# Attention kernel with top-2 experts: routing spread between the maxima of attention, map entries and the transposition of the maxima placed elsewhere

## The reference, cut to what matters

```python
xn = layernorm(x)                                   # x: [4, 1024, 256]
# attention: 16 heads of 16, causal, ALiBi bias, softmax
q, k, v = xn @ Wq, xn @ Wk, xn @ Wv
scores = (mask(q @ k.T) + slope * (j - i)) / sqrt(16)
attn = (softmax(scores) @ v) @ Wo + bo
# router: two experts of eight for each token
r = xn * rsqrt(mean(xn**2) + 1e-6) * 256**-0.5 * router_scale
logits = r @ router_logits
probs = softmax(logits);  choices = top_2(logits)
weights = probs / sum(probs of the two)
# experts: rows sorted by expert, gelu(x @ gate) * (x @ up), @ down, times per-expert scale
out = x + attn + sum_k weights[k] * expert[choices[k]](xn)
```

## Time and profile before

| | us |
|---|---|
| median of 3 runs (931.12 to 932.04) | 931.17 |
| the profiled execution | 941.12 |
| its span | 939.4 |
| TensorE busy, share of the span | 812.5, 86% |
| VectorE | 562.1, 60% |
| ScalarE | 483.2, 51% |
| GpSimd | 390.0, 42% |

### The profile page before, as it was taken

How to read it: one execution, slowest core, us unless ns; L and a number is a source line. 1 busy time by engine, 2 the same in 40 slices (tenths; PEclk the granted TensorE clock), 3 DMA queues, 4 the chain that set the end, 5 groups by cost and what they waited for, 6 DMA issues and landing times. The chain is left out here.

```text
span 939.4 us, 17505 instructions
## 1 busy us (share of the span) xinstructions
PE 812.5 (86%) x5618; PEld 426.3 (45%) x5619; DVE 562.1 (60%) x1560; ACT 483.2 (51%) x1011; POOL 390.0 (42%) x456
## 2 busy tenths in 40 slices
PE   5989601799999999999999999856999999999598
PEld 2555400134444444444444444313555656555497
DVE  4767364988888888888888888301222222222177
ACT  2333300067777777777777777852333333333374
POOL 3545340033223233322323332323666666665398
PEclk9999855589999999999999999996999999999799
DMA  4999899295555666555566600009222222222485
GB/s 157 221 263 269 213 107 121 34 253 74 62 61 57 82 81 81 67 62 61 59 82 81 81 3 3 2 6 321 86 84 84 84 84 84 84 85 78 129 245 182
DMA packets 115004, 100.32 MB, mean 107 GB/s; under 512 B 58172, under 2 KB 95676, under 8 KB 114876
## 3 DMA queue, kind: packets, MB, share of 16 engines
q1 hardware_dynamic: 105976, 80.50, 46.9%
q0 software_dynamic: 8960, 18.95, 6.4%
HBM read 63.89 MB, written 35.00 MB: 105 GB/s over the span
## 5 line engine op out<-in xcount | busy, mean ns | idle before, releaser
L784 ACT ACTIVATE probs<-spsum 128x512 f32<-128x512 f32 x576 | 312.1, 604 | 169.6 <-PE spsum L835 163.8
L742 DVE CUSTOM_DVE_ANT_0 junk<-mpsum,mask 128x128 bf16<-128x128 f32 (+7 forms) x512 | 360.0, 754 | 58.5 <-issue 51.7
L824 PE MATMUL mpsum<-ks,qs 102*128 102x512 bf16 (+3 forms) x768 | 183.5, 343 | 45.9 <-DVE cpsum L731 26.3
L722 POOL TENSOR_SCALAR_AFFINE_SELECT probs<-probs 128x512 f32<-128x512 f32 x128 | 78.8, 634 | 340.8 <-ACT probs L784 340.8
L835 PE MATMUL spsum<-qs,ks 105*128 105x512 bf16 (+3 forms) x768 | 199.2, 329 | 10.6 <-ACT probs L784 8.3
L855 PE MATMUL cpsum<-probs,vs 128*17 128x256 f32 (+2 forms) x2560 | 152.7, 360 | 1.5 <-POOL probs L722 0.8
L1037 PE MATMUL gu<-w_gu,xTs 128*128 x288 | 139.2, 607 | 1.7 <-ACT xTs L981 1.7
L1016 DVE COPY hT<-hp 128x256 f32<-128x256 f32 x72 | 30.6, 425 | 167.8 <-PE hp L1044 100.6
L824 PEld LDWEIGHTS mpsum<-ks,qs 102*128 102x128 bf16 x768 | 69.8, 100 | 122.5 <-DVE maxima L742 39.8
L835 PEld LDWEIGHTS spsum<-qs,ks 105*128 105x128 bf16 x768 | 67.1, 97 | 102.9 <-ACT probs L784 52.9
L956 POOL DMA_INDIRECT expert_rows<-y,places x72 | 70.7, 983 | 72.2 <-ACT y L990 42.2
(11 more groups left out here) (124 smaller groups left out, 698.5 us busy)
## 6 DMA issues: line engine op xcount, KB each, us to landing
qk_parts<-parts SPq DMA_DIRECT2D x32, 384.0 KB, 4.4
qs<-qk_parts SPq DMA_DIRECT2D x96, 128.0 KB
ks<-qk_parts SPq DMA_DIRECT2D x96, 128.0 KB
yk<-expert_rows SPq DMA_DIRECT2D x32, 256.0 KB, 3.1
v_rows<-vt SPq DMA_DIRECT2D x32, 136.0 KB, 4.5
vs<-v_rows SPq DMA_DIRECT2D x16, 272.0 KB, 12.0
x_in<-in_x SPq DMA_DIRECT2D x8, 512.0 KB, 6.3
xn_rows<-xn SPq DMA_DIRECT2D x8, 512.0 KB, 5.8
```

Source lines behind the costliest of these rows:

```text
L722: pool.affine_select(out=part, in_=part, compare_op=ALU.is_ge, fill=0.0, base=0, pattern=[[0, 4], [1, P]], channel_multiplier=-1).then_inc ...
L742: last = dve.tensor_tensor_reduce(junk[:, slot, c:c + w], mpsum[:, slot, c:c + w], keep["mask"][:, S - w:S], 1.0, 3 * NEG, ALU.add, ALU.ma ...
L784: act.activation(probs[:, u % PRING, h], spsum[:, (4 * u + h) % SRING], ACT.Exp, scale=SCALE).then_inc(exp_done, 1)
L824: last = pe.matmul(mpsum[:, slot, at + c:at + e], qs[hq][0:R_MAX, h, qt * P:(qt + 1) * P], ks[hq][0:R_MAX, h, c:e], start=True, stop=True)
```

## The change

The block `route` is gone; its parts stand elsewhere.

- Projection: no hardware loop, four x buffers instead of two, one store of v per chunk for all quads, and the scale of the logits is computed per chunk by GpSimd (three more small operations) and applied by ScalarE. GpSimd sets up the constants of the routing and the mask between its first and second chunk. SyncE loads the constant rows of all quads at the start, and the first quad in pieces behind the stores of chunks 2 to 5.
- Attention: VectorE takes one piece of the routing after the item of each odd pair: 49 pieces, 45 in steps 0 to 4 and 4 in step 5. The counts are an item of their own in pair 10 of step 1 and are copied out of PSUM. ScalarE takes its exponential ahead of unit 5 of step 1.
- The transposed maxima go into a buffer of the ring of scores, not of maxima, once per step; a score that comes later to that buffer waits for `t_taken`.
- GpSimd writes the map in steps 5 to 12, two DMAs behind each of units 6, 7, 8 and 0, straight from the kept tiles. SyncE loads `w_gu` in eight parts in the same steps (its place holds the routing's tiles until then, which is why they are printed as `w_gu` below) and reads the map back at the end of attention.

```diff
+COUNT_AT = (1, 10)
+SOFTMAX_AT = (1, 5)
+MAP_FROM = 5
+MAP_UNITS = (6, 7, 8, 9)
...
+def score_slots():
+    p, = [p for p, pair in enumerate(PAIR_ITEMS) if (1, NI - 1) in pair]
+    seq = [("T", 0)] + [("S", 0, h) for h in range(4)]
+    for n in range(1, B * NQ * NU):
+        t, j = (n - 1) // NU, (n - 1) % NU + 1
+        for h in range(4):
+            seq.append(("S", n, h))
+            if p // 2 + 1 == j and 2 * (p % 2) == h and t + 1 < B * NQ:
+                seq.append(("T", t + 1))
+    return seq, {user: i for i, user in enumerate(seq)}
...
-                for q in range(NQ):
-                    sp.dma_start(scratch["v"][q].rearrange("(t p) w -> p t w", p=P)[:, ds(4 * c, 4), :],
-                                 vt[:, par, :, q].rearrange("p t h w -> p t (h w)")).then_inc(v_stored[par], 16)
+                sp.dma_start(scratch["v"].rearrange("(t p) w -> p t w", p=P)[:, 4 * c:4 * c + 4, :],
+                             vt[:, par].rearrange("p t q h w -> p t (q h w)")).then_inc(v_stored[par], 16)
...
+            for c in range(NC):
+                stores(c, c % 2, c + XR < NC)
+                if c == 2:
+                    sp.wait_ge(parts_stored[0], 16 + 16 * 2)
+                if 2 <= c < 5:
+                    load_rows(sp, scratch, heads, 0, 0, (2 * c - 4, 2 * c - 3))
+                if c == 5:
+                    for i in range(2):
+                        sp.wait_ge(v_stored[i], 16 * 2)
+                    load_values(sp, scratch, heads, 0, 0)
...
+            load_quad(sp, scratch, heads, 0, 1)
             maxima_rows(0, 0)
+            load_quad(sp, scratch, heads, 0, 2)
...
+                if t == MAP_FROM:
+                    sp.wait_ge(routed, 1)
+                if MAP_FROM <= t < MAP_FROM + NE:
+                    e = t - MAP_FROM
+                    sp.dma_start(keep["w_gu"][:, e * DH:(e + 1) * DH], ins["w_gu"][:, e * DH:(e + 1) * DH]).then_inc(keep["w_gu_in"], 16)
...
-                    if j == LOW_LAST[0]:
-                        map_entries(b, hq)
+                    if j in MAP_UNITS and t >= MAP_FROM:
+                        map_entries(NU * t + j, len(MAP_UNITS) * (t - MAP_FROM) + MAP_UNITS.index(j))
...
+            def map_entries(n, part):
+                wait_apart(pool, exp_done, 4 * n + SRING)
+                wait_apart(pool, routed, 1)
+                for e in range(2 * part, min(2 * part + 2, 2 * NT)):
...
+                def then(ins_):
+                    ins_.then_inc(dve_step, 1)
+                    steps[0] += 1
+                    dve.wait_ge(dve_step, steps[0])
...
+                for p in range(PAIRS):
+                    if (t, p) == COUNT_AT:
+                        count_item()
+                    for j, k in PAIR_ITEMS[p]:
                         if has(j):
                             item(t + j, (hq + j) % NQ, k)
+                    if p % 2 == 1:
+                        next(route, None)
```

More of the change, by code:

```diff
@@ L38 @@
 NC = TOK // CH
+XR = 4
 NST = 2 * TOK // P + NE
@@ new lines, in load_quad, with __init__, __call__ @@
+def load_quad(sp, scratch, heads, b, hq):
+    load_rows(sp, scratch, heads, b, hq, range(len(Q_PART)))
+    load_values(sp, scratch, heads, b, hq)
+class Room:
+    def __init__(self, buffer):
+        self.words, self.at = buffer, 0
+    def __call__(self, shape, dt=F32):
+        n = math.prod(shape[1:]) // (2 if dt is BF16 else 1)
+        part = self.words[0:shape[0], self.at:self.at + n]
+        self.at += n
+        if dt is not F32:
+            part = part.bitcast(dt)
+        dims = "abcde"[:len(shape) - 1]
+        return part.rearrange(f"p ({' '.join(dims)}) -> p {' '.join(dims)}", **dict(zip(dims, shape[1:])))
@@ L192, in project @@
         passed = sem("passed1")
-        x_loaded = [sem(f"x_loaded{i}") for i in range(2)]
+        x_loaded = [sem(f"x_loaded{i}") for i in range(XR)]
         x_stored = [sem(f"x_stored{i}") for i in range(2)]
@@ L243, in _ @@
             sp.dma_start(w_qk[:, :, :, :], ins["w_qk"]).then_inc(weights_in, 16)
-            sp.dma_start(x_in[:, 1], x_rows[1]).then_inc(x_loaded[1], 16)
+            for i in range(1, XR):
+                sp.dma_start(x_in[:, i], x_rows[i]).then_inc(x_loaded[i], 16)
             def stores(c, par, load):
@@ L621, in attend @@
         mparts = sb("mparts", [12 * KT, 2, P], BF16)
-        entries = sb("entries_now", [P, 2, 2, 2, 2], I32)
-        slots = sb("slots", [P, 2, 2, 2], I32)
+        room, early = keep["w_gu_room"], keep["route"]
+        rank_of, tile_no, reset, ones, tri = (early[name] for name in ("rank_of", "tile_no", "reset", "ones", "tri"))
+        logit, escale = keep["logits"][:, :, :], keep["escale"]
+        hit, key, masked_l, expd, prob, picked = (room([P, NT, NE]) for _ in range(6))
+        chosen = [room([P, NT, NE]) for _ in range(2)]
+        cnt, run, pos = (room([P, NE, NT]) for _ in range(3))
+        both = room([P, NT, NE], BF16)
+        counts = [room([P, NT * NE]) for _ in range(2)]
+        past = room([1, NST, NE])
+        first, esum, renorm, guard, sk, slot_f = (room([P, NT]) for _ in range(6))
+        top, pk = ([room([P, NT]) for _ in range(2)] for _ in range(2))
+        slot_i = room([P, 3, NT], I32)
+        total, tiles, ends, base = (room([P, NE]) for _ in range(4))
+        total_i, tiles_i = (room([P, NE], I32) for _ in range(2))
+        tile_f = room([1, NST])
         mpsum = ctx.enter_context(nc.psum_tensor("mpsum", [P, 2, S], F32))
@@ L641, in attend @@
         ctx_taken = sem("ctx_taken")
-        entries_in = [sem(f"entries_in{i}") for i in range(2)]
-        entries_out = [sem(f"entries_out{i}") for i in range(2)]
+        entries_out = sem("entries_out")
+        dve_step = sem("dve_step_r")
+        shifted = sem("shifted")
+        exp_ready = sem("exp_ready")
+        both_ready = sem("both_ready")
+        routed = sem("routed")
         block = ctx.enter_context(nc.Block())
@@ L759, in _, with count_item @@
+            def count_item():
+                n = ITEM_NO[COUNTS]
+                dve.wait_ge(m_taken, n + 1)
+                wait_apart(dve, m_ready, n + 1)
+                for j in range(2):
+                    last = dve.tensor_copy(counts[j], mpsum[:, n % RING, CH * j:CH * j + NT * NE])
+                last.then_inc(m_taken, 1)
+            route = routing()
             for k in range(NI - 1):
@@ new lines, in item, with score_buffer, count_item @@
+                last.then_inc(m_ready, 1)
+            def score_buffer(*user):
+                i = SCORE_AT[user] - SRING
+                if i >= 0 and SCORE_SEQ[i][0] == "T":
+                    pe.wait_ge(t_taken, SCORE_SEQ[i][1] + 1)
+                elif i >= 0:
+                    pe.wait_ge(exp_done, 4 * SCORE_SEQ[i][1] + SCORE_SEQ[i][2] + 1 + SRING)
+            def count_item():
+                n = ITEM_NO[COUNTS]
+                pe.wait_ge(both_ready, 1)
+                pe.wait_ge(m_taken, n + 1)
+                for j, which in enumerate((tri, ones)):
+                    last = pe.matmul(mpsum[:, n % RING, CH * j:CH * j + NT * NE], which, both,
+                                     start=True, stop=True)
+                last.then_inc(m_ready, 1)
@@ L935, in _ @@
             sp.sem_inc(y_free, RR)
-            sp.dma_start(places[:, :, :].rearrange("p s c -> p (s c)"), scratch["map"].rearrange("(p s) c -> p (s c)", p=P)).then_inc(places_in, 16)
             for e in range(NE):
```

446 lines of the change are left out of this document (203 added, 243 removed).

## The result

| | before | after |
|---|---|---|
| median, beside each other (4 runs each) | 931.61 | 894.89 |
| from, to | 931.12 to 932.3 | 894.28 to 897.78 |
| ratio, 95% interval | | 0.9604 (0.9586 to 0.9622) |
| the profiled execution | 941.12 | 894.28 |
| its span | 939.4 | 892.5 |

The forecast was 902.0 us (885 to 914), the result 894.89. The profiled execution of before lay 10 us above its other runs, that of after lies among its own; so the two spans differ by 46.9 us and the medians by 36.7. Chips differ too: the runs that follow were made in three sets, each on one chip, and the kernel before took 938.08, 941.81 and 935.03 us in them.

The account below looks back on a forecast made before the run. TensorE's order was taken to bound the kernel, its two holes being the quick gains. Terms -42.5 - 1.9 + 15 + 7.2 + 0 - 6.9 were summed to -29.2: profiled 911.9, median 902 us, range 885 to 914.

Parts of the forecast that it names:

- the hole: Between projection and attention: 48.0 us, mostly routing alone on VectorE, become 5.5, so -42.5 us.
- routing: Attention steps 0 to 5: pieces want 38.1 us of VectorE, 23.1 fit its idle time, so +15 us.
- map entries: Steps 5 to 12: entry pairs delay the mask of unit 1, TensorE waits 0.9 us eight times, +7.2 us.
- the stretch behind attention: Attention to experts: -3.8 entries landing earlier, -2.1 gather not behind map load, -1 gather before weights; -6.9 us.
- the projection: Projection: four x buffers remove VectorE's wait, -2.6; GpSimd's late reciprocal root costs about 0.7; -1.9 us in all.
- The bound of 12.3 us for the first quad: Projection: upper bound on what loading the first quad there costs in DMA time; 0 was taken.
- the handover of 0.33 us: Routing steps: each of 49 pieces delays the next VectorE item by 0.33 us, read behind the transposition.
- Rival B: Steps 0 to 5: handovers vanish, routing's 21.9 us fit in 23.1 of idle time; 887 us, chance 13%.
- Pieces in contention with masks: Routing steps: two-input VectorE pieces slowed by GpSimd masks, some 2 us more; counted as nothing.
- rival C: Steps with map entries: masks come in time, as pairs are shorter or TensorE has slack; 895 us, chance 13%.
- The transposition: Each attention step: freeing the maxima buffer removes TensorE's 0.92 us wait, but VectorE starts no earlier; 0 us.
- wait of about 0.9 two items later: Attention steps: sign that TensorE's wait behind the transposition only moves two items later, about 0.9 us.

## Why the prediction was right, and where it was wrong

The range held, and that is in part luck: the forecast's error of 7.1 us is what is left of two larger ones that point in opposite directions. By the profiled spans the sum should have been -29.2 (its terms add up to -29.1) and was -46.9, a miss of 17.7 us, more than the 17 us from the forecast to the range's lower end. Against it, the 9.95 us by which the profiled execution of before exceeded its median were carried over to the kernel after, whose profiled execution has no such surplus (894.28 against a median of 894.89). The largest term, the hole, was right in mechanism and size; routing, map entries and the stretch behind attention were not.

| term | forecast | by the traces |
|---|---|---|
| between projection and attention | -42.5 | -44.3 |
| projection (last logits at 107.94) | -1.9 | -2.1 |
| routing, steps 0 to 5 | +15 | +7.9 (0.6 and 7.3) |
| entries and transposition, steps 6 to 13 | +7.2 | -3.2 |
| steps 14 and 15 | 0 | -1.1 |
| behind attention | -6.9 | -2.1 |
| experts and combination | 0 | -2.1 |

*The hole and the projection* held. The bound of 12.3 us for the first quad was empty: its cost was 0 and, had it been left at attention's start, 15.3.

*Routing*: the step that failed is the handover of 0.33 us. That row stands behind the transposition, where VectorE's sequencer executes two increments between the wait and the item; behind a piece it executes one, and that handover measured 0.22. With that the sum's own working gives 21.2 + 0.84 + 49 x 0.22 = 32.8 us into 23.1, +9.7, near the +7.9. The mechanism was right: without the handovers 8.8 us come back. Rival B, which wanted them hidden, was wrong about them; the work without them does fit. Pieces in contention with masks, which the sum left at nothing, added nearly nothing: two of them met one (the one at 266.48 took 0.90 us instead of 0.42, one at 153.81 took 0.75), 0.8 us in all, but the 21.10 of the earlier trace rows held such a meeting too, and the busy time is 21.2.

*Map entries*: the mechanism was right, a weight load of TensorE waits for the late mask of unit 1. The step that failed is the time from the mask of unit 7 to that of unit 1, forecast as 10.1 to 10.6 us and measured as 9.8. The pairs took 2.24 as forecast; the changes between mask and pair were shorter, a mask following an entry in 0.02 us and not in 0.16. TensorE lost 0.17 us a step, not 0.9: rival C, on that chip. On the other chip a step with entries took 0.83 us more than there, and by its rows with another mechanism than the one forecast.

*The transposition*: 0 in the routing steps, 0.25 us in each other step of the changed kernel, and nothing measurable in the time of either kernel. The reason given (VectorE does not start earlier) is what the traces show for the items; the "wait of about 0.9 two items later" came as 0.70.

What remains of the shorter steps (27.11 against 27.52, while 0.25 are the transposition's and the entries cost 0.17) is about the wait of 0.23 to 0.30 us for an exponential that stood in each of the steps 1 to 13 of before:

```profile
262.74 0.39 PE L835 MATMUL spsum<-qs,ks 105*128 105x512 bf16 x1 [0.28 <-ACT probs L784]
```

In the steps of after it doesn't stand, with the transposition in its old buffer either. But it is not the change's alone: in the kernel before with only the transposition moved it is absent on one chip (steps of 26.95) and 0.12 to 0.17 us on the other (27.24 to 27.29), and in the kernel before on that other chip mostly 0.12 to 0.21. What sets it was not isolated.

*Behind attention*: the step that failed is -3.8 for the landing of the last entries. Something did hold the block until 4 us after ScalarE's end, but it was GpSimd's drain, which the change leaves in place; the wait of 4.3 us at that barrier in the earlier trace rows was put down to the entries' landing, which no row there shows, while the drain in that same trace runs until 632.13, just before SyncE's 632.45. The other two parts, forecast as -3.1, gave -2.1.

*Experts*: the term was put at nothing. The granted clock is 0.81 in their first 14.4 us, where it was 0.63 in the 14.6 us of before: the lower level (0.50, 1.2 GHz), which sets in during the hole, in which TensorE does nothing, lasts some 5 us into the experts after and some 11 us before. That goes with the 2.1 us, but why it ended earlier is open. It is not the length of the hole: in the run with the deferred waits the hole is 10.3 us as in the changed kernel, the clock of that stretch 0.64, and the experts take 238.6 us as before.

```profile
595.63:610.00 14.37, 12.66 (x36) 6.07 (x37) 2.01 (x5) 4.55 (x10) 2.89 (x3) 0.81 1.06 347
...
640.45:655.00 14.55, 12.84 (x29) 5.89 (x30) 2.03 (x5) 3.97 (x8) 1.89 (x2) 0.63 1.08 348
```

## What to carry to other kernels

When a chain of small operations is laid between the work of a busy engine, the handover counts as much as the operations: let each piece wait at its start for the one before, signal another engine from the operation itself, and count what the sequencer has to execute behind a wait. When a barrier ends late, look for the engine that arrives last and what its sequencer does there, and don't take a DMA for the cause that no row shows. A forecast that carries the surplus of one profiled execution over to another kernel takes over an error of that size.

## What the runs showed that was not expected

*GpSimd's drain.* After a block with indirect DMAs it took until 5.3 us behind the last mask, though the last of them had been issued some 70 us before; without them 0.1 us. At the end of the experts it lasted 3.16 us, and TensorE's wait there fell by 3.15 without it. Leaving it out gave back both; what the drain does in that time no run shows.

*Two-input operations beside masks.* With the handovers gone, pieces met masks more often: nine operations with two tensors, two of which had met one before, took 0.73 to 0.87 us where they take 0.42 alone, or 0.50 to 0.55 where they take 0.19, every one of them while a mask ran (the one at 181.03 above took 0.42 in the changed kernel). One with a single input took 0.35 instead of 0.17. Another with two tensors, at 205.97, kept its 0.41, and there the pair of masks took 1.47 us instead of 1.23. Reductions beside a mask kept their 0.41. The 59 operations were 23.8 us busy instead of 21.2. The Trainium skill ("SBUF — State Buffer", Who interferes with whom) states both, that an instruction with two SBUF inputs contends with a reading GpSimd instruction and that a reduction never does; the traces agree. The rule that changed nothing in the sum is worth 2.6 us of VectorE's time once the handovers are gone.

*Chips differ inside a step.* The changed kernel on the other chip: GpSimd's masks and ScalarE's exponentials near the end of a step with entries.

```profile
429.86 1.22 POOL L644 TENSOR_SCALAR_AFFINE_SELECT probs<-probs 128x512 f32<-128x512 f32 x2
433.49 0.65 POOL L644 TENSOR_SCALAR_AFFINE_SELECT probs<-probs 128x512 f32<-128x512 f32 x1
...
430.47 2.07 ACT L825 ACTIVATE probs<-spsum 128x512 f32<-128x512 f32 x4 [0.93 <-PE spsum L898]
434.12 0.60 ACT L825 ACTIVATE probs<-spsum 128x512 f32<-128x512 f32 x1 [1.59 <-PE spsum L898]
```

TensorE's records up to there lie as on the first chip, counted from the mask of unit 7. But the exponentials at 430.47 and 434.12 start 0.33 and 1.1 us later than there, each within 0.04 us of the end of a mask operation (the first row holds two, the second row ends at 433.49 + 0.65), in all of steps 5 to 12, and so again in the run without the drain on that chip. ScalarE waits for no mask in the code, and the rows say that its waits ended with TensorE's signal: in the trace's semaphore events that signal itself comes 0.33 and 1.1 us late, 0.02 us before either exponential, while the ends of TensorE's records are modelled. So it is TensorE's scores that come late there. The cause is open; the kernel without entries was not run on that chip.
